# A kernel's setup joined to its main block: coefficient steps, row sums and g moved among other work

## Chip, cores and metric

One Trainium2 chip, one core of it. The metric is the device time of one execution in microseconds. Five engines with their own instruction queues work side by side: PE (matrix products), ACT, DVE and POOL (elementwise work), SP (issues the DMAs). Each queue runs strictly in order; they meet by semaphores.

## What is computed

Two graph layers with a layer norm before each, in float32, for 16 batches of 512 nodes by 128 features:

```python
h = maximum(layernorm(x), 0);  x = x + gnn0(h, adj)
h = maximum(layernorm(x), 0);  x = x + gnn1(h, W, adj)
# gnn0: eight Euler steps of an ODE
h = x0 @ fc_in_w.T + fc_in_b
f = sigmoid(alpha) * 0.5 * (adj @ h - h) + h @ (w * clip(d, 0, 1) @ w.T) - h + x0
h = h + f / 8
# gnn1: attention with 4 heads of 32, scores masked where adj == 0
```

The eight Euler steps are linear in x0. The kernel writes one step as h <- P h + h Q + x0/8, where P holds the adjacency scaled by rows and a diagonal, and Q the w part. Then h after eight steps is a sum over powers of P of terms with 128x128 coefficient matrices R_k (made by eight steps of a recurrence with Q), and a part g that comes from the bias fcb and the row sums of P's powers. The coefficients are taken three at a time, which needs P to the powers one and two as matrices and the cube P^3 for the outer steps.

## The kernel before

Every float32 matrix that enters a large product is kept as a high part (pH, u0_h, rH, wH: a copy on ACT to a shorter format) and a low part (pL, u0_l, rL, wL: a subtraction on DVE or POOL), and a product is three products: high by high, low by high, high by low. So a bank of PSUM that PE has filled is drained twice, by ACT (high) and then by DVE (low, which reads the high part).

The program has two blocks. In the first (`setup_block`, L215 to L502) each engine gets one function; the block ends when all five have ended. In the second, `ode_stage` and `attention_stage` follow each other in each engine's function. PSUM banks and SBUF of the setup are given back behind its block and used again by the ODE: ps_p0 to ps_p3 become ps_u and ps_v, ps_c and ps_w become ps_z and ps_k.

The setup, in order on PE. *Head*: transposes to keep warm (L88); the turn of w (L434); for each of four row blocks of the adjacency, which DVE scales (L367) and gives its diagonal (L369), four transposes (L439) into ps_p; then Q (L444). ACT makes the high part of P itself (p_h, L314), POOL the low part (p_l, L297). *Powers*: eight groups, n = 0 to 7, `power(1, 0..3)` and `power(2, 0..3)`. A group is twelve products (L459, L462, L465) into ps_p[m], drained by ACT (L323) and DVE (`low`, L390). Ahead of group n stands coefficient step n: n + 1 coefficients against Q, three to a product (L473) into ps_c, which DVE adds to the coefficients of the step before (`step`, L398 and L402). Among these stand the first layer norm's parts for the ODE's first four batches: on DVE the statistics (L116, L126; parts 0 and 1, in even n) and reciprocal and scaling (L138, L146; parts 2 and 3, in odd n), on ACT the root (L133, even n) and the relu with the high part of u (L200, L203, odd n), on POOL its low part (L211). DVE's order in a group is step, norm, low, and for part 3 behind low. *End*: the row sums of the powers (sixteen products with three columns, L482) in ps_w, the turns of the bias column into c_rows (L491, to ps_p[3]) and of the nine coefficient matrices (L496, to ps_p), copies s_rows (DVE), c_rows and rH (ACT) and rL (DVE), and g, the product of s_rows and c_rows (L501), which ACT copies (L342).

The ODE stage runs over groups of four batches; group 0 is written out ahead of a loop. For each batch PE makes `u_step` (four transposes of u0, L1140, then twice twelve products with the powers, L95 to L97) into three banks, which ACT and DVE drain; and one batch behind, `v_step`: products with rH and rL, to which DVE adds g (L1083). Products with the cube follow (`z_step`, `y_step`), and work for the next stage stands among them. Attention follows batch by batch.

Of the kernel before, what the change touches and what calls it, by code (L numbers as in the profile page):

```python
# [214 lines left out]
def setup_block(nc, ctx, x, adj, alpha, w, d, fcw, fcb, wqkv, keep, ln):  # L215
# [3 lines left out]

    def sem(name):  # L220
        return ctx.enter_context(nc.semaphore(name))
# [29 lines left out]
    p_done, ph_done, pl_done = (sem(n) for n in ("p_done", "ph_done", "pl_done"))  # L251
    pow_mm, pow_h, pow_l = (sem(n) for n in ("pow_mm", "pow_h", "pow_l"))
    w_mm, w_done, table_in = sem("w_mm"), sem("w_done"), sem("table_in")
    coef_mm, coef_done, coef_ready = sem("coef_mm"), sem("coef_done"), sem("coef_ready")
    r_mm, r_h, r_l = sem("r_mm"), sem("r_h"), sem("r_l")
    row_mm, row_done, g_mm, g_done = (sem(n) for n in ("row_mm", "row_done", "g_mm", "g_done"))
# [3 lines left out]

    def bank_g(t):

        return ps_c[:, t, 0:3 * D] if t < 3 else ps_p[3][:, 0:3 * D]

    block = ctx.enter_context(nc.Block())

    @block.sync
    def _(sp):
# [11 lines left out]
    @block.gpsimd  # L280
    def _(pool):
# [19 lines left out]
    @block.scalar  # L301
    def _(act):
# [5 lines left out]
        act.dma_start(d_sb[:, :], d.rearrange("(p o) -> p o", o=1)).then_inc(w_in, 16)  # L308
# [24 lines left out]
        act.wait_ge(row_mm, 2)  # L333
        act.activation(c_rows[:, :], ps_p[3][0:3, 0:3 * D], ACT.Copy).then_inc(row_done, 1)

        for j in range(3):
            act.wait_ge(r_mm, j + 1)
            act.activation(keep["rH"][:, j, :], ps_p[j][:, 0:3 * D], ACT.Copy).then_inc(r_h, 1)

# [4 lines left out]
    @block.vector  # L344
    def _(dve):
# [9 lines left out]

        dve.wait_ge(exp_done, 1)
# [5 lines left out]
        dve.wait_ge(ident_done, 2)  # L362
        for t in range(T):
# [8 lines left out]
        dve.wait_ge(w_in, 32)  # L372
# [3 lines left out]
        dve.tensor_copy(w_t[:, :], ps_w[:, 0:D])  # L376
        dve.tensor_scalar(w_td[:, :], ps_w[:, 0:D], d_dt[:, 0:1], None, ALU.mult).then_inc(w_done, 1)
        dve.wait_ge(w_mm, 2)
        dve.tensor_copy(q_sb[:, :], ps_w[:, 0:D]).then_inc(w_done, 1)

        dve.wait_ge(coef_zero, 2)
        for c in coef:
            dve.tensor_scalar(c[:, 0, 0:D], ident[:, :], DT, None, ALU.mult).then_inc(coef_ready, 1)
# [22 lines left out]

        for m in range(T):
            low(0, m)
        for n in range(STEPS):
            step(n)  # L410

            for part in (0, 1) if n % 2 == 0 else (2,):
                first_norm_dve(dve, ln, 0, n // 2, part)
            low(1 + n // T, n % T)
            if n % 2:
                first_norm_dve(dve, ln, 0, n // 2, 3)

        dve.wait_ge(qw_h, 1)
        dve.tensor_tensor(keep["wL"][:, :], w_qkv[:, :], keep["wH"][:, :].bitcast(F32),
                          ALU.subtract).then_inc(qw_l, 1)  # L420

        dve.wait_ge(row_mm, 1)
        dve.tensor_scalar(s_rows[:, :], ps_w[0:3, :], ident[0:3, 0:1], None, ALU.add).then_inc(row_done, 1)
        for j in range(3):
            dve.wait_ge(r_h, j + 1)
            dve.tensor_tensor(keep["rL"][:, j, :], ps_p[j][:, 0:3 * D], keep["rH"][:, j, :].bitcast(F32),
                              ALU.subtract).then_inc(r_l, 1)

    @block.tensor
    def _(pe):  # L430
        pe.wait_ge(ident_done, 2)
        keep_warm(pe, ps_p[0], ident, WARM_START)
        pe.wait_ge(w_in, 32)
        pe.transpose(ps_w[:, 0:D], w_sb[:, :], ident[:, :]).then_inc(w_mm, 1)  # L434

        for t in range(T):
# [5 lines left out]

        pe.wait_ge(w_done, 1)
        pe.matmul(ps_w[:, 0:D], w_td[:, :], w_t[:, :], start=True, stop=True).then_inc(w_mm, 1)  # L444
        pe.wait_ge(w_done, 2)
        pe.wait_ge(f_in, 32)
        pe.wait_ge(coef_zero, 2)
        pe.wait_ge(coef_ready, 2)

# [18 lines left out]
        for n in range(STEPS):  # L468
            if n:
                pe.wait_ge(coef_done, n)  # L470
            for s in range(1, n + 2, 3):
                k = min(3, n + 2 - s)
                mm = pe.matmul(ps_c[:, (s - 1) // 3, 0:k * CW], q_sb[:, :],  # L473
                               coef[n % 2][:, s:s + k, :].rearrange("p k c -> p (k c)"), start=True, stop=True)
            mm.then_inc(coef_mm, 1)
            power(1 + n // T, n % T)

        pe.wait_ge(pick_done, 3)
        for j in range(2):
            for m in range(T):  # L480
                for part in ("pH", "pL"):
                    mm = pe.matmul(ps_w[0:3, :], pick[:, j, :], keep[part][j][:, m, :],  # L482
                                   start=(j == 0 and m == 0 and part == "pH"),
                                   stop=(j == 1 and m == T - 1 and part == "pL"))
        mm.then_inc(row_mm, 1)

        fin = coef[STEPS % 2]
        pe.wait_ge(coef_done, STEPS)
        pe.wait_ge(pow_l, 3 * T)
        for i in range(3):  # L490
            tr = pe.transpose(ps_p[3][0:3, i * D:(i + 1) * D], fin[:, 1 + 3 * i:4 + 3 * i, D], ident[:, :])  # L491
        tr.then_inc(row_mm, 1)

        for j in range(3):
            for i in range(3):
                tr = pe.transpose(ps_p[j][:, i * D:(i + 1) * D], fin[:, 1 + 3 * i + j, 0:D], ident[:, :])  # L496
            tr.then_inc(r_mm, 1)

        pe.wait_ge(row_done, 2)
        for t in range(T):  # L500
            pe.matmul(bank_g(t), s_rows[:, t * 128:(t + 1) * 128], c_rows[:, :],  # L501
                      start=True, stop=True).then_inc(g_mm, 1)  # L502


def ode_stage(nc, ctx, sem, x, adj, x1_dram, qk_dram, v_dram, keep, ln):
# [213 lines left out]
    def sync(sp):  # L719
# [4 lines left out]
        def v_step(g, b, following):  # L724
# [3 lines left out]
            wait(sp, xv_done, GB * g + b)  # L728
            sp.dma_start(x_res[:, :, :], batch_of(x, GB * g + b).rearrange("o (p t) d -> p (o t) d", t=T)).then_inc(xr_in, 16)
# [118 lines left out]
    def scalar(act):  # L848
        def u_step(g, b, prev):
            for k in range(3):  # L850
# [148 lines left out]
    def vector(dve):  # L999
# [74 lines left out]
        def v_step(g, b, following):  # L1074
            for t in range(T):
                n = T * (GB * g + b) + t
                wait(dve, v_mm, n + 1)
                if t == 0:
# [46 lines left out]
    def tensor(pe):  # L1125
        def u_step(g, b, prev):

            nb = GB * g + b
            for k in range(3):
                n = 3 * nb + k  # L1130
                ps = u_bank(b, k)

# [15 lines left out]
        def v_step(g, b, following):  # L1148

            nb = GB * g + b  # L1150
            wait(pe, ul_done, 3 * nb + 3)
            for t in range(T):
# [413 lines left out]
def graph_block(nc, x, adj, alpha, w, d, fcw, fcb, wqkv, out):  # L1566
# [4 lines left out]
    with ExitStack() as outer:  # L1571
# [13 lines left out]
        with ExitStack() as kept:  # L1585
# [6 lines left out]
            with ExitStack() as ctx:  # L1592
                setup_block(nc, ctx, x, adj, alpha, w, d, fcw, fcb, wqkv, keep, ln)
            ode_ctx = kept.enter_context(ExitStack())
            ode = ode_stage(nc, ode_ctx, sem, x, adj, x1_dram, qk_dram, v_dram, keep, ln)
        with ExitStack() as ctx:
# [4 lines left out]
            def _(sp):  # L1601
                ode.sync(sp)
# [3 lines left out]
            def _(pool):  # L1606
                ode.gpsimd(pool)
# [3 lines left out]
            def _(act):  # L1611
                ode.scalar(act)
# [3 lines left out]
            def _(dve):  # L1616
                ode.vector(dve)
# [3 lines left out]
            def _(pe):  # L1621
                ode.tensor(pe)
# [21 lines left out]
```

## Time and profile before

| | us |
|---|---|
| median of 3 runs | 688.59 (686.69 to 688.61) |
| profiled execution | 685.76, span 684.0 |
| first block, to the first transposes of the ODE | 0 to 55.2 |
| its matrix powers on PE | 14.3 to 46.4 |
| attention | from about 390 |

The profile's times count from the first instruction of the profiled execution. In a row of the timeline, a name such as "[0.83 <-PEq L1592]" is the time that the engine sat idle ahead of the instruction and what ended it. PE's products overlap, so their durations sum to more than the time from one start to the next; starts are the better measure. The granted clock is 1.00 at 2.4 GHz and 0.50 at 1.2 GHz.

### The profile page before, as it was taken

What the parts mean: (1) busy time and instruction counts of PE and PEld (TensorE: products, weight loads), DVE (VectorE), ACT (ScalarE), POOL (GpSimd) and SP (SyncE); (2) the same over time, 40 slices, a digit from 0 to 9 for tenths busy, and PEclk for the clock granted to TensorE, in tenths of its full rate; (3) what the DMA queues carried; (4) which work ended last, traced back from release to release, by engine and by line L of the source; (5) the groups of instructions that cost most, each with busy time, mean ns of one, the idle gap of its engine ahead of it and who ended that gap; (6) DMA issues with size and microseconds to landing.
All of it is one profiled execution on the core that took longest, in us unless ns stands there. A gap on an engine that the chain in (4) does not pass through costs nothing.

```text
span 684.0 us, 13068 instructions
## 1 busy us (share of the span) xinstructions
PE 646.0 (94%) x3737; PEld 501.9 (73%) x3737; DVE 481.2 (70%) x1331; ACT 398.9 (58%) x923; POOL 130.6 (19%) x112
## 2 busy tenths in 40 slices
PE   6999999999899998999999778999999999999996
PEld 4767997789778897788987656666666666666663
DVE  6662563377833777336653569999999999999993
ACT  3433232124541345412232559999999999999994
POOL 5110235012330133301133910000000000000001
PEclk8999999999999999999999999999999999999999
DMA  3101110211235111350037896677777777777710
GB/s 111 32 0 47 32 31 16 72 40 60 75 150 170 42 58 74 147 173 13 25 109 218 181 409 191 149 180 172 175 173 177 174 176 171 177 176 177 183 58 32
DMA packets 48656, 82.53 MB, mean 121 GB/s; under 512 B 5104, under 2 KB 13680, under 8 KB 48496
## 3 DMA queue, kind: packets, MB, share of 16 engines
q1 hardware_dynamic: 48192, 82.07, 44.8%
q8 instruction: 16, 0.26, 0.2%
q14 instruction: 16, 0.13, 0.1%
q10 hardware_dynamic: 432, 0.07, 0.1%
HBM read 52.76 MB, written 29.36 MB: 120 GB/s over the span
## 4 chain that ended last, share of the span: by engine, by line
PE 30%; issue 20%; ACT 4%; POOL 4%; DVE 2%; POOLq 0%; DVEq 0%; ACTq 0%
PE ps_t L1517 13%; PE ps_o L1548 7%; PE ps_s L1532 7%; ACT v L1467 1%; ACT p_t L1458 1%; POOL z_l L831 1%; POOL h L715 1%; PE ps_o L1555 1%; POOL v L824 1%; DVE v L1489 1%; ACT ut L896 0%; DVE low L1489 0%; DVE p_t L1483 0%; PE ps_u L95 0%; PE ps_u L97 0%
## 5 line engine op out<-in xcount | busy, mean ns | idle before, releaser
L1467 ACT ACTIVATE v<-v,low 128x512 f32<-128x512 f32 x256 | 182.4, 716 | 7.0 <-DVE low L1489 6.7
L1489 DVE CUSTOM_DVE_ANT_0 v<-ps_s,pL 128x512 f32<-128x512 f32 x256 | 165.6, 685 | 11.8 <-PE ps_s L1532 11.1
L1517 PE MATMUL ps_t<-ident,v 128*128 128x128 f32 x1024 | 155.0, 274 | 4.8 <-ACT p_t L1458 4.2
L1517 PEld LDWEIGHTS ps_t<-ident,v 128*128 128x128 f32 x1024 | 123.2, 140 | 33.1 <-DVE p_t L1483 8.8
L1532 PE MATMUL ps_s<-pL,pH 128*128 128x512 f32 x256 | 122.8, 481 | 2.3 <-DVE low L1489 2.0
L1483 DVE COPY p_t<-ps_t 128x512 f32<-128x512 f32 x128 | 85.0, 685 | 0.9 <-PE ps_t L1517 0.9
L1458 ACT ACTIVATE p_t<-ps_t 128x512 f32<-128x512 f32 x128 | 74.4, 583 | 0.3 <-PE ps_t L1517 0.3
L1445 POOL TENSOR_TENSOR o_n<-o_n,x 128x512 f32<-128x512 f32 x16 | 20.6, 1286 | 265.6 <-DVE o_n L1499 265.6
L1532 PEld LDWEIGHTS ps_s<-pL,pH 128*128 128x128 f32 x256 | 48.3, 189 | 30.4 <-DVE low L1489 17.4
L95 PE MATMUL ps_v<-rH,ut 128*128 128x384 f32 x192 | 65.1, 339 | 4.6 <-DVE v L1083 4.6
L1548 PE MATMUL ps_o<-p_t,v_sb 128*32 128x512 f32 x512 | 61.4, 597 | 4.6 <-issue 3.6
L97 PE MATMUL ps_v<-rH,ut 128*128 128x384 f32 x192 | 64.6, 336 | 0.0
L96 PE MATMUL ps_v<-rL,ut 128*128 128x384 f32 x192 | 64.5, 336 | 0.0
L855 ACT ACTIVATE ut<-ps_u 128x512 fp32r<-128x512 f32 x44 | 26.1, 594 | 65.1 <-PE ps_u L97 43.6
L1008 DVE TENSOR_TENSOR ut<-ps_u,ut 128x512 fp32r<-128x512 f32 x44 | 30.3, 688 | 36.2 <-ACT ut L855 36.1
L819 POOL TENSOR_TENSOR v_l<-v,v_h 128x512 fp32r<-128x512 f32 x16 | 21.0, 1312 | 176.9 <-ACT v_h L961 176.9
L1083 DVE TENSOR_TENSOR v<-ps_v,g 128x384 f32<-128x384 f32 x64 | 35.5, 556 | 26.7 <-PE ps_v L97 25.7
L1467 ACT ACTIVATION_READ_ACCUMULATOR v<-v,low 128x1 f32 x256 | 49.2, 192 | 0.0
L95 PE MATMUL ps_u<-pH,u_h 128*128 128x512 f32 x112 | 46.0, 410 | 0.0
L97 PE MATMUL ps_u<-pH,u_l 128*128 128x512 f32 x112 | 44.3, 395 | 0.0
L96 PE MATMUL ps_u<-pL,u_h 128*128 128x512 f32 x112 | 44.2, 394 | 0.0
L961 ACT ACTIVATE v_h<-v 128x512 fp32r<-128x512 f32 x16 | 10.1, 633 | 52.8 <-DVE v L1083 52.8
(208 smaller groups left out, 1102.0 us busy)
## 6 DMA issues: line engine op xcount, KB each, us to landing
pH<-qk_dram SPq DMA_DIRECT2D x64, 256.0 KB, 6.8
pL<-qk_dram SPq DMA_DIRECT2D x64, 256.0 KB, 7.6
qk_dram<-qk SPq DMA_DIRECT2D x12, 512.0 KB, 3.3
x_ln<-in_x SPq DMA_DIRECT2D x16, 256.0 KB, 3.1
x_res<-in_x SPq DMA_DIRECT2D x16, 256.0 KB, 2.6
x_dram<-v SPq DMA_DIRECT2D x16, 256.0 KB, 3.1
v_sb<-v_dram SPq DMA_DIRECT2D x16, 256.0 KB, 9.3
x<-x_dram SPq DMA_DIRECT2D x16, 256.0 KB, 9.4
```

Of the source, the lines that this page charges most:

```text
L95: eng.matmul(psum, lh, rh, start=(first and n == 0), stop=False)
L96: eng.matmul(psum, lh, rl, start=False, stop=False)
L97: mm = eng.matmul(psum, ll, rh, start=False, stop=(last and n == len(pairs) - 1))
L1008: dve.tensor_tensor(ut_l[b % 2][:, k, :], u_bank(b, k)[:, :], ut_h[b % 2][:, k, :].bitcast(F32), ALU.subtract).then_inc(ul_done, 1)
L1083: dve.tensor_tensor(v[:, :, t, b, :], ps_v[t % 2][:, 0:3 * D].rearrange("p (j d) -> p j d", j=3), keep["g"][:, t, :].rearrange("p (j d) -> ...
L1458: act.activation(dst, src, ACT.Copy).then_inc(t_act, 1)
L1467: act.activation(s_ring[:, n % RING, :], s_ring[:, n % RING, :], ACT.Exp, bias=low[:, n:n + 1], scale=-1.0, accum_out=lsum[par][:, n:n + 1 ...
L1483: dve.tensor_copy(dst, src).then_inc(t_dve, 1)
L1489: dve.tensor_tensor_reduce(s_ring[:, n % RING, :], ps_s[S_BANK[n]][:, :], mask[:, n // HEADS, :], -SCALE, 3.0e38, ALU.add, ALU.min, low[:, ...
L1517: mm = pe.transpose(ps_t[n % T_BANKS][:, j * 128:(j + 1) * 128], s_ring[:, n % RING, j * 128:(j + 1) * 128], ident[:, :])
L1532: pe.matmul(ps_s[S_BANK[n]][:, :], q_st[par][:, h, it * 128:(it + 1) * 128], k_st[par][:, h, :], start=True, stop=True).then_inc(s_mm, 1)
L1548: mm = pe.matmul(ps_o[cols, :], v_sb[cp][:, j, cols], p_t[cp][:, hh, j, :], start=(j == 0), stop=(j == T - 1), tile_position=(0, HD * hh))
```

## The change

Setup's five programs are put ahead of the ODE's in the one block; so no engine waits for all others between them, and where memory is used twice, waits on the last user are added. On PE: w's turn waits for w alone; Q is made between row blocks two and three; coefficient steps 0 and 1 stand ahead of the powers, and step n + 2 behind group n; the row sums stand behind group 4; the turns stand behind group 6, those of the coefficients first and in ps_c, and the last group waits until ACT has copied c_rows from ps_p[3]; g is made at the head of `u_step` of the second batch. On DVE: the identity's scalings go ahead of all, the w work goes between row blocks two and three, `step(0)` stands ahead of the first low parts, and in a group the order is low, step, norm. POOL waits for all four row blocks before its first subtraction. ACT copies rH and c_rows behind the high part and root of group 6. SP's loads of the bias weights wait for one zeroed buffer only.

```diff
-        sp.wait_ge(coef_zero, 2)
+        sp.wait_ge(coef_zero, 1)
...
+        pool.wait_ge(p_done, T)
         for t in range(T):
             pool.wait_ge(ph_done, t + 1)
...
+                if (k, m) == GROUPS[COEF_AT]:
+                    for j in range(3):
+                        act.wait_ge(r_mm, j + 1)
+                        act.activation(keep["rH"][:, j, :], ps_c[:, j, 0:3 * D], ACT.Copy).then_inc(r_h, 1)
+                    act.wait_ge(row_mm, 2)
+                    act.activation(c_rows[:, :], ps_p[3][0:3, 0:3 * D], ACT.Copy).then_inc(row_done[1], 1)
...
+        rows(0)
+        rows(1)
+        dve.wait_ge(d_in, 16)
         col(dve.tensor_scalar(d_dt[:, :], d_sb[:, :], 0.0, 1.0, ALU.max, ALU.min))
...
+        rows(2)
+        rows(3)
...
+        step(0)
         for m in range(T):
             low(0, m)
-        for n in range(STEPS):
-            step(n)
-
-            for part in (0, 1) if n % 2 == 0 else (2,):
+        step(1)
+        for n, (k, m) in enumerate(GROUPS):
+            low(k, m)
+            if n + EARLY < STEPS:
+                step(n + EARLY)
+
+            for part in (0, 1) if n % 2 == 0 else (2, 3):
                 first_norm_dve(dve, ln, 0, n // 2, part)
...
+        for n, (k, m) in enumerate(GROUPS):
+            if n == len(GROUPS) - 1:
+                pe.wait_ge(row_done[1], 1)
+            power(k, m)
+            if n + EARLY < STEPS:
+                coef_step(n + EARLY)
+            if n == ROWS_AT:
+                row_sums()
+            if n == COEF_AT:
+                coef_turns()
...
+            if isinstance(g, int) and (g, b) == (0, 1):
+                keep["tensor_g"](pe)
...
+                if isinstance(g, int) and (g, b) == (0, 0):
+                    wait(pe, keep["powers"], 2 * T + k + 1)
...
             def _(pe):
+                setup.tensor(pe)
                 ode.tensor(pe)
                 attention.tensor(pe)
```

Here EARLY is 2, ROWS_AT 4 and COEF_AT 6; row_sums, coef_turns and coef_step hold the products of L482, L491 with L496, and L473.

## Rows read from the trace of the kernel before

**Rows 1.** Page, part 1: engine, busy us (share of span), instructions.

```profile
PE 646.0 (94%) x3737; PEld 501.9 (73%) x3737; DVE 481.2 (70%) x1331; ACT 398.9 (58%) x923; POOL 130.6 (19%) x112
```

**Rows 2.** Windows, ODE stage: stretch, length, busy us (instructions) by engine, granted clock, DMA.

```profile
120.00:140.00 20.00, 20.00 (x91) 16.09 (x92) 7.98 (x22) 3.19 (x7) 1.17 (x1) 1.00 0.30 93
```

**Rows 3.** Timeline, head, DVE: start, us, engine, line, operation, out<-in, shape.

```profile
6.62 0.70 DVE L367 TENSOR_SCALAR p_nat<-a_nat,s_col 128x512 f32<-128x512 f32 x1
...
7.63 1.69 DVE L367 TENSOR_SCALAR p_nat<-a_nat,s_col 128x512 f32<-128x512 f32 x1
9.35 1.24 DVE L369 SCALAR_TENSOR_TENSOR p_nat<-ident,c_col,p_nat 128x128 f32<-128x128 f32 x1
...
11.24 0.35 DVE L369 SCALAR_TENSOR_TENSOR p_nat<-ident,c_col,p_nat 128x128 f32<-128x128 f32 x1
...
12.09 0.34 DVE L377 TENSOR_SCALAR w_td<-ps_w,d_dt 128x128 f32<-128x128 f32 x1
```

**Rows 4.** One line, POOL's subtractions: ns min/median/max, first and last start.

```profile
L297 POOL TENSOR_TENSOR p_l<-p_nat,p_h x4: 1253/1386/1645, 7.5 to 12.7; 128x512 fp32r<-128x512 f32 x4
```

**Rows 5.** Timeline, the powers, all engines.

```profile
19.20 0.59 PE L473 MATMUL ps_c<-coef,q_sb 128*128 128x258 f32 x2
...
20.01 1.28 ACT L133 ACT_TABLE_LOAD   x1
...
38.97 0.59 DVE L146 TENSOR_SCALAR u<-x_ln,ln_mv,ln_std 128x128 f32<-128x128 f32 x2
...
40.26 0.63 ACT L203 ACTIVATE u_h<-u 128x512 fp32r<-128x512 f32 x1
...
40.75 0.86 DVE L116 BATCH_NORM_STATS2 ln_stat<-x_ln 128x6 f32<-128x128 f32 x4
...
41.76 0.38 DVE L126 BATCH_NORM_AGGREGATE ln_mv<-ln_stat 128x2 f32<-128x6 f32 x4
41.86 1.90 PE L473 MATMUL ps_c<-coef,q_sb 128*128 128x387 f32 x6
42.06 0.60 ACT L323 ACTIVATE pH<-ps_p 128x512 fp32r<-128x512 f32 x1 [1.16 <-PE ps_p L465]
42.55 0.29 ACT L133 ACTIVATE ln_std<-ln_mv,eps 128x4 f32<-128x4 f32 x1
42.69 0.69 DVE L390 TENSOR_TENSOR pL<-ps_p,pH 128x512 fp32r<-128x512 f32 x1 [0.55 <-ACT pH L323]
...
43.80 1.36 DVE L402 TENSOR_TENSOR coef<-ps_c,coef 128x387 f32<-128x387 f32 x3 [0.28 <-PE ps_c L473]
```

**Rows 6.** Timeline, end of the block and first ODE batch.

```profile
46.40 0.40 PE L482 MATMUL ps_w<-pH,pick 128*3 128x512 f32 x1
...
50.13 0.49 PE L491 MATMUL ps_p<-ident,coef 128*3 128x128 f32 x3
...
50.66 0.48 ACT L334 ACTIVATE c_rows<-ps_p 3x384 f32<-3x384 f32 x1 [0.90 <-PE ps_p L491]
51.05 1.20 ACT L338 ACTIVATE rH<-ps_p 128x384 fp32r<-128x384 f32 x3
...
51.53 2.20 PE L501 MATMUL ps_c<-c_rows,s_rows 3*128 3x384 f32 x6
...
55.21 0.83 PE L1140 MATMUL ps_u<-ident,u 128*128 128x128 f32 x4 [0.83 <-PEq L1592]
...
62.74 0.60 PE L1140 MATMUL ps_u<-ident,u 128*128 128x128 f32 x4
```

**Rows 7.** Windows of 1 us; the last figures are granted clock, DMA share, GB/s.

```profile
55.00:56.00 1.00, 0.79 (x5) 0.82 (x6) 0.00 (x0) 0.00 (x0) 0.00 (x0) 0.74 0.00 0
56.00:57.00 1.00, 1.00 (x4) 0.80 (x3) 0.29 (x1) 0.60 (x1) 0.00 (x0) 0.50 0.50 113
57.00:58.00 1.00, 1.00 (x4) 0.71 (x4) 0.40 (x1) 0.00 (x0) 0.00 (x0) 0.50 0.87 313
58.00:59.00 1.00, 1.00 (x4) 0.81 (x3) 0.00 (x0) 0.00 (x0) 0.00 (x0) 0.55 0.59 184
```

More of the change, by code:

```diff
@@ L212, in first_norm_pool, with setup_stage @@
                        ALU.subtract).then_inc(ln.u0l_done, 1)
-def setup_block(nc, ctx, x, adj, alpha, w, d, fcw, fcb, wqkv, keep, ln):
+def setup_stage(nc, ctx, sem, x, adj, alpha, w, d, fcw, fcb, wqkv, keep, ln):
     def sb(name, shape, dt=F32):
         return ctx.enter_context(nc.sbuf_tensor(name, shape, dt))
-    def sem(name):
-        return ctx.enter_context(nc.semaphore(name))
     a_nat = sb("a_nat", [128, T, N])
@@ L278, in _, with gpsimd @@
                 sp.dma_start(w_qkv[:, :], wqkv).then_inc(q_in, 16)
-    @block.gpsimd
-    def _(pool):
+    def gpsimd(pool):
         pool.memset(ln.norm.eps[:, :], EPS).then_inc(ln.eps_done, 1)
@@ L299, in _, with scalar @@
             first_norm_pool(pool, ln, 0, b)
-    @block.scalar
-    def _(act):
+    def scalar(act):
         act.dma_start(alpha_sb[:, :], alpha.rearrange("(p t) -> p t", t=T)).then_inc(alpha_in, 16)
@@ L307, in _ @@
         act.dma_start(w_sb[:, :], w).then_inc(w_in, 16)
-        act.dma_start(d_sb[:, :], d.rearrange("(p o) -> p o", o=1)).then_inc(w_in, 16)
+        act.dma_start(d_sb[:, :], d.rearrange("(p o) -> p o", o=1)).then_inc(d_in, 16)
         act.wait_ge(alpha_in, 16)
@@ L331, in _, with scalar_g @@
                     first_norm_act(act, ln, 0, n // 2)
[L333 to L338, printed above, removed]
+                if (k, m) == GROUPS[COEF_AT]:
[4 more added lines that the diff above has]
+                    act.activation(c_rows[:, :], ps_p[3][0:3, 0:3 * D], ACT.Copy).then_inc(row_done[1], 1)
+    def scalar_g(act):
         for t in range(T):
@@ L342, in _, with vector @@
             act.activation(keep["g"][:, t, :], bank_g(t), ACT.Copy).then_inc(g_done, 1)
-    @block.vector
-    def _(dve):
+    def vector(dve):
         n_col = 0
@@ L353, in col @@
             dve.wait_ge(col_done, n_col)
+        dve.wait_ge(ident_done, 2)
+        dve.wait_ge(coef_zero, 2)
+        for c in coef:
+            dve.tensor_scalar(c[:, 0, 0:D], ident[:, :], DT, None, ALU.mult).then_inc(coef_ready, 1)
         dve.wait_ge(exp_done, 1)
@@ L360, in _, with rows @@
         col(dve.tensor_scalar(c_col[:, :], s_col[:, :], -1.0, 1.0 - DT, ALU.mult, ALU.add))
-        dve.wait_ge(ident_done, 2)
-        for t in range(T):
+        def rows(t):
             dve.wait_ge(adj_in[t], 16)
@@ L405, in step, with tensor, rows @@
             last.then_inc(coef_done, 1)
+        step(0)
         for m in range(T):
             low(0, m)
-        for n in range(STEPS):
-            step(n)
-            for part in (0, 1) if n % 2 == 0 else (2,):
-                first_norm_dve(dve, ln, 0, n // 2, part)
[L414 to L430, printed above, removed]
+        step(1)
[4 more added lines that the diff above has]
+            for part in (0, 1) if n % 2 == 0 else (2, 3):
+                first_norm_dve(dve, ln, 0, n // 2, part)
+            if n == ROWS_AT:
+                dve.wait_ge(row_mm, 1)
+                dve.tensor_scalar(s_rows[:, :], ps_w[0:3, :], ident[0:3, 0:1], None, ALU.add).then_inc(row_done[0], 1)
+                dve.wait_ge(qw_h, 1)
+                dve.tensor_tensor(keep["wL"][:, :], w_qkv[:, :], keep["wH"][:, :].bitcast(F32),
+                                  ALU.subtract).then_inc(qw_l, 1)
+            if n == COEF_AT:
+                for j in range(3):
+                    dve.wait_ge(r_h, j + 1)
+                    dve.tensor_tensor(keep["rL"][:, j, :], ps_c[:, j, 0:3 * D], keep["rH"][:, j, :].bitcast(F32),
+                                      ALU.subtract).then_inc(r_l, 1)
+    def tensor(pe):
         pe.wait_ge(ident_done, 2)
         keep_warm(pe, ps_p[0], ident, WARM_START)
-        pe.wait_ge(w_in, 32)
+        pe.wait_ge(w_in, 16)
         pe.transpose(ps_w[:, 0:D], w_sb[:, :], ident[:, :]).then_inc(w_mm, 1)
-        for t in range(T):
+        def rows(t):
             pe.wait_ge(p_done, t + 1)
@@ L441, in _, with coef_step @@
                     tr.then_inc(pow_mm, 1)
+        def coef_step(n):
+            if n:
+                pe.wait_ge(coef_done, n)
+            for s in range(1, n + 2, 3):
+                k = min(3, n + 2 - s)
+                mm = pe.matmul(ps_c[:, (s - 1) // 3, 0:k * CW], q_sb[:, :],
+                               coef[n % 2][:, s:s + k, :].rearrange("p k c -> p (k c)"), start=True, stop=True)
+            mm.then_inc(coef_mm, 1)
+        rows(0)
+        rows(1)
         pe.wait_ge(w_done, 1)
         pe.matmul(ps_w[:, 0:D], w_td[:, :], w_t[:, :], start=True, stop=True).then_inc(w_mm, 1)
+        rows(2)
+        rows(3)
         pe.wait_ge(w_done, 2)
@@ L448, in _ @@
         pe.wait_ge(coef_ready, 2)
+        coef_step(0)
+        coef_step(1)
         def power(k, m):
@@ L466, in power @@
             mm.then_inc(pow_mm, 1)
[L468 to L491, printed above, removed]
@@ L492, in _, with row_sums @@
-        tr.then_inc(row_mm, 1)
-        for j in range(3):
-            for i in range(3):
-                tr = pe.transpose(ps_p[j][:, i * D:(i + 1) * D], fin[:, 1 + 3 * i + j, 0:D], ident[:, :])
-            tr.then_inc(r_mm, 1)
-        pe.wait_ge(row_done, 2)
+        def row_sums():
+            pe.wait_ge(pick_done, 3)
+            pe.wait_ge(pow_l, 2 * T)
+            for j in range(2):
+                for m in range(T):
+                    for part in ("pH", "pL"):
+                        mm = pe.matmul(ps_w[0:3, :], pick[:, j, :], keep[part][j][:, m, :],
+                                       start=(j == 0 and m == 0 and part == "pH"),
+                                       stop=(j == 1 and m == T - 1 and part == "pL"))
+            mm.then_inc(row_mm, 1)
@@ new lines, in coef_turns @@
+        def coef_turns():
+            fin = coef[STEPS % 2]
+            pe.wait_ge(coef_done, STEPS)
+            for j in range(3):
+                for i in range(3):
+                    tr = pe.transpose(ps_c[:, j, i * D:(i + 1) * D], fin[:, 1 + 3 * i + j, 0:D], ident[:, :])
+                tr.then_inc(r_mm, 1)
+            pe.wait_ge(pow_l, 2 * T)
+            for i in range(3):
+                tr = pe.transpose(ps_p[3][0:3, i * D:(i + 1) * D], fin[:, 1 + 3 * i:4 + 3 * i, D], ident[:, :])
+            tr.then_inc(row_mm, 1)
@@ L500, in _, with tensor_g @@
+        for n, (k, m) in enumerate(GROUPS):
[4 more added lines that the diff above has]
+                coef_step(n + EARLY)
+            if n == ROWS_AT:
+                row_sums()
+            if n == COEF_AT:
+                coef_turns()
+    def tensor_g(pe):
+        for s in row_done:
+            pe.wait_ge(s, 1)
         for t in range(T):
+            if t < 3:
+                pe.wait_ge(r_l, t + 1)
@@ L501, in _ @@
             pe.matmul(bank_g(t), s_rows[:, t * 128:(t + 1) * 128], c_rows[:, :],
                       start=True, stop=True).then_inc(g_mm, 1)
+    keep["scalar_g"], keep["tensor_g"], keep["g_done"] = scalar_g, tensor_g, g_done
+    keep["powers"], keep["weights"] = pow_l, [(r_l, 3), (qw_l, 1)]
+    keep["adj_read"] = (p_done, T)
+    return Programs(sync, gpsimd, scalar, vector, tensor)
 def ode_stage(nc, ctx, sem, x, adj, x1_dram, qk_dram, v_dram, keep, ln):
@@ L728, in v_step @@
             wait(sp, xv_done, GB * g + b)
+            if isinstance(g, int) and (g, b) == (0, 0):
+                wait(sp, *keep["adj_read"])
             sp.dma_start(x_res[:, :, :], batch_of(x, GB * g + b).rearrange("o (p t) d -> p (o t) d", t=T)).then_inc(xr_in, 16)
@@ L849, in u_step @@
         def u_step(g, b, prev):
+            if isinstance(g, int) and (g, b) == (0, 1):
+                keep["scalar_g"](act)
             for k in range(3):
@@ L1077, in v_step @@
                 wait(dve, v_mm, n + 1)
+                if t == 0 and isinstance(g, int) and (g, b) == (0, 0):
+                    wait(dve, keep["g_done"], T)
                 if t == 0:
@@ L1128, in u_step @@
             nb = GB * g + b
+            if isinstance(g, int) and (g, b) == (0, 1):
+                keep["tensor_g"](pe)
             for k in range(3):
@@ L1131, in u_step @@
                 ps = u_bank(b, k)
+                if isinstance(g, int) and (g, b) == (0, 0):
+                    wait(pe, keep["powers"], 2 * T + k + 1)
                 if (b, k) == (0, 2):
@@ L1151, in v_step @@
             wait(pe, ul_done, 3 * nb + 3)
+            if isinstance(g, int) and (g, b) == (0, 0):
+                wait(pe, keep["powers"], 3 * T)
+                for s, value in keep["weights"]:
+                    wait(pe, s, value)
             for t in range(T):
@@ L1592, in graph_block @@
             with ExitStack() as ctx:
-                setup_block(nc, ctx, x, adj, alpha, w, d, fcw, fcb, wqkv, keep, ln)
+                setup = setup_stage(nc, ctx, sem, x, adj, alpha, w, d, fcw, fcb, wqkv, keep, ln)
             ode_ctx = kept.enter_context(ExitStack())
@@ L1601, in _ @@
             def _(sp):
+                setup.sync(sp)
                 ode.sync(sp)
@@ L1606, in _ @@
             def _(pool):
+                setup.gpsimd(pool)
                 ode.gpsimd(pool)
@@ L1611, in _ @@
             def _(act):
+                setup.scalar(act)
                 ode.scalar(act)
@@ L1616, in _ @@
             def _(dve):
+                setup.vector(dve)
                 ode.vector(dve)
```

24 lines of the change are left out of this document (12 added, 12 removed).

## The prediction

> **What bounds the kernel now.** I read the busy shares first. TensorE (PE) is busy 94% of the span [rows 1], and a stretch of the ODE stage shows it full while DVE, ACT and POOL are not [rows 2]. So up to the attention stage PE's order sets the time, and what PE loses or wins in the setup is carried to the end one for one, as far as I can read. The change touches only the first 63 us, so I read the timeline there, engine by engine. The reader is to see three things in it. In the head, DVE scales the rows of the adjacency, and the third and fourth row block take 1.69 and 1.24 us for what takes 0.70 and 0.35 elsewhere, while POOL is in its four subtractions [rows 3, 4]. In the matrix powers PE has no gap: 27.20 us pass from 19.20 to 46.40 [rows 5, 6]. At the end come PE's row sums, turns and g, then 0.83 us of idle PE at the end of the block [rows 6], and then the granted clock is 0.74, 0.50, 0.50 and 0.55 in the microseconds from 55 to 59, that is, at the 1.2 GHz level from 55.5 to 58.9 [rows 7].
>
> Two marks carry the comparison: PE is free behind the first group of powers at 19.20 (call this zero), and the second batch of the ODE begins at 62.74 [rows 5, 6]. Between them lie 43.54 us of PE. From 41.86 to 46.40 stand eight coefficients and a group, from 19.20 to 46.40 thirty-five and seven groups; that gives 0.215 us for a coefficient and 2.8 for a group. So the 43.54 are: coefficients 7.5, seven groups 19.6, row sums 3.73 (46.40 to 50.13), turns 1.40 (50.13 to 51.53), g 2.85, idle 0.83, and 7.53 for the first batch's products, of which 3.4 us at half clock lost 1.7.
>
> **Head: gain 1.8.** POOL now waits for all four row blocks, so DVE's two slow steps lose 0.99 + 0.89 = 1.88 us. Four small operations on d and w (0.92 us: from 11.51, by the view 0.27 behind the start of the last diagonal step, to 12.43) come in between. The fourth row block, at 11.59 before, is done at 11.59 - 1.88 + 0.92, about 10.6 [rows 3]. POOL then does its four subtractions in a row, at 1.25 us or a little more each (the shortest of [rows 4]); with one DVE step between, they end at about 15.9. The group's first products can begin at about 13.3, behind the first coefficient step and the first low part, but its eighth needs the last subtraction. Five products follow from 15.9, at 0.23 us (2.8 / 12) at full clock or nearly twice that at half, so PE is free at 17.1 to 18.0. Upper bound: at half clock throughout, 13.35 + 12 x 0.43 = 18.5. I take 17.4, a gain of 1.8 (0.7 to 2.1). The two scalings of the identity go ahead of DVE's first wait and cost nothing there; the earlier loads on SP's queue are awaited later than they land.
>
> A page that bears here is the Trainium skill's SBUF — State Buffer, section "Who interferes with whom": a DVE operation that uses the pair of ports shared with GpSimd locks it for a whole instruction, and the loser waits it out. The slow steps above agree. By that rule the copy at the head of the first coefficient step would wait out a subtraction too and take a turn of 0.2 us between two; without it the gain of the head would be about 2.0.
>
> **The powers: cost 1.1, less 0.4.** One coefficient step is now ahead of zero, so 0.43 us go (2 x 0.215). Otherwise PE has the same products in another order. What is new is the order on DVE and ACT: the norm's parts stand behind the low part and the coefficient step of the same group, not ahead of the low part. From zero, with durations of rows 5: high part 0.2 to 0.8; low 1.44; step 2.04; statistics and aggregate 1.39, to 3.43. ACT now waits for that before its root. Its function table load (1.28) stands directly ahead of the root, behind the wait in program order; no row shows a load against an unmet wait, so its price is between 0 and 1.28, and I take all of it. Root done at 5.05; the second high part at 5.0, though PE had finished at 3.44. Then low and step 7.0, reciprocal and four scalings 8.3, relu and high part of u (0.67 + 0.63) 9.65. Third group: PE done at 7.1, its high part at 9.65, step done at 11.9. PE's next coefficient step, due at 11.0, waits for that: 0.9 lost. The fourth high part is done at 14.05, just late for the fifth group: 0.15. Behind that the row sums give DVE and ACT 3.73 us to catch up. Bounds 0 to 1.5; I take 1.1 for the three together with 0.03 of waiting before.
>
> **The seventh group: cost 4.6 and 1.5.** Here the moved work makes a new wait. The last group may not start until ACT has copied c_rows out of its bank, and PE makes c_rows' turns only behind the seventh group (index 6). ACT is late: the relu and high part for the third batch keep it until 1.34 behind the end of that group (28.7). From 30.06: high part 0.60, low part 0.61 to its successor, statistics and aggregate of the fourth batch 1.39, root 0.3, the three rH copies (1.17 to the next), c_rows 0.48, with handovers 4.6, to 34.66 [rows 5, 6]. PE has its twelve turns (1.33) in that time and is done at 30.04. It waits 4.62 us. Behind ACT's wait for the root stand rH and c_rows; behind rH stands DVE's rL; PE has nothing else in its queue. The order alone sets a floor: were ACT free at once, 3.4 would be left; doubling of the lateness gives 6.
>
> The clock fell after 0.83 us of idle PE in the trace [rows 6, 7], and stayed up in the gapless powers. Behind 4.6 idle us I take it down again, for a time like the one read, with 1.5 lost in the last group (0 to 3.4, that is none or twice the 1.7 read). TensorE: Matmul & The Clock Gate, section "HAM oscillation — how this bites in real kernels", of the Trainium skill says that a wait between bursts of matmuls throttles the next burst. The trace agrees (0.83 us idle, then half clock); without that rule and row the 1.5 would be 0.
>
> **End of the block and ODE: gain 2.8.** The idle 0.83 goes. The first batch's products follow the last group at once, at full clock or nearly: 5.83 in place of 7.53. g (2.6 for 2.85) comes behind them. ACT reaches the first batch's copies only behind the fourth batch's relu, about 4.2 us behind the last group, but PE needs a drained bank only for the second batch, 8.4 behind it; so 2 us of cover are left, and if g were faster or ACT later, the difference would be paid. g's copies on ACT (four of about 0.5) are needed by the first addition on DVE, two batches of products later. The x loads of SP go out earlier and are needed later.
>
> **Sum.** 7.1 + 19.6 + 1.1 + 3.73 + 1.33 + 4.62 + 1.5 + 5.83 + 2.6 = 47.4 in place of 43.5: 3.9 more, 1.8 less at the head: 2.1 us longer. The profiled execution took 685.76 (span 684.0 and 1.8 around it), so 687.9 by that basis; it was faster than all runs shown (median 688.59). I add the difference to the median: 690.7.
>
> **Rivals.** First, not slower: DVE and ACT keep up. Place: the table load and ACT's relu of the third batch; price 1.1 (the stalls in the powers) and 1.2 (the lateness at the seventh group). It decides if ACT has finished that relu before group seven ends. For it: DVE and ACT are idle much of the powers in the present order. Against: the chain of low, step, statistics and root is serial. It gives 2.1 - 2.3, so 688.4; with the clock staying up too, 686.9. Second, worse: g's three-row products, now amid the ODE, bring the clock down once more. For it: the fall at 55.5 came behind them, with only 0.83 idle. Against: full products now stand right behind them. It costs 1.7: 692.4; with the row sums doing the same in the powers, 694.1. Third, the join is worth more than its visible idle, because the block's end also holds back engines that the PE view does not show; ODE then would run 2 to 3 us ahead of my sum and the kernel would be faster, 685.9 at best. I see no row that says so. Last, the join hides nothing, because ACT's lateness reaches the second batch: 2 us of cover would have to go; 692 or so.
>
> **Chances.** My forecast (689 to 692) 0.45; the first rival 0.27; the second and the last together 0.18; the third 0.10. This kernel's measurements tell about 0.3% (2.06 us) from no change. My forecast lies on that edge, so it goes half to slower, half to same. Faster 0.13 (the third and a little of the first), same 0.46, slower 0.41. Range: 685.8 (the first rival with the clock up, and most of the third) to 695.0 (the second with both falls, and the upper bound of the head); the forecast's own 689 to 692.
>
> **What would show it.** In the trace of the changed kernel: DVE's four row scalings at 0.70, POOL's first subtraction behind the fourth; PE free behind the first group near 17.4; an idle PE of 4 to 5 us between the turns and the last group's products, released by ACT's c_rows; half clock right behind it; no gap between last group and first ODE transposes. The second batch's transposes at 64.8 confirm the sum. I am wrong if that idle is under 3 us, if c_rows comes ahead of the fourth batch's root, or if stretches behind 65 us change in length.

## The result and the profile after

The changed kernel took 691.39 us (median of 4, 690.31 to 692.07) against 688.43 for the kernel before: ratio 1.0047, 95% interval 1.0025 to 1.007. It is 3.0 us (0.5%) slower. The profiled execution took 690.31 (span 688.5) against 685.76 (684.0), so 4.5 us longer; both lie below their medians, the one of before by more.

The page's first part answers to [rows 1]: the same instructions, hardly other busy times.

```profile
PE 648.7 (94%) x3737; PEld 503.1 (73%) x3737; DVE 481.3 (70%) x1331; ACT 398.2 (58%) x923; POOL 130.0 (19%) x112
```

The head, in DVE's timeline rows and POOL's and PE's, answers to [rows 3, 4]:

```profile
8.27 0.67 DVE L372 TENSOR_SCALAR p_nat<-a_nat,s_col 128x512 f32<-128x512 f32 x1
...
8.97 0.35 DVE L374 SCALAR_TENSOR_TENSOR p_nat<-ident,c_col,p_nat 128x128 f32<-128x128 f32 x1
...
10.40 4.98 POOL L298 TENSOR_TENSOR p_l<-p_nat,p_h 128x512 fp32r<-128x512 f32 x4 [6.45 <-DVE p_nat L374]
10.44 1.32 DVE L403 COPY coef<-coef 128x129 f32<-128x129 f32 x1
...
12.61 2.26 PE L481 MATMUL ps_p<-pH,p_h 128*128 128x512 f32 x4
...
16.94 0.81 PE L455 MATMUL ps_c<-coef,q_sb 128*128 128x387 f32 x2
```

The row blocks are back at 0.67 and 0.35, and PE is free behind the first group at 16.94 instead of 19.20. The group began at 12.61; in the kernel before it began at 14.95:

```profile
14.95 2.07 PE L459 MATMUL ps_p<-pH,p_h 128*128 128x512 f32 x4
...
16.00:17.00 1.00, 1.00 (x4) 0.81 (x3) 1.00 (x5) 0.00 (x0) 0.00 (x0) 0.50 0.00 0
```

It took about as long in both, 4.33 and 4.25 us, and in both the granted clock (the third figure from the end of a row of windows) was 0.50 for most of it: from 11.1 to 17.9 before, from 12.1 to 15.5 in the changed kernel:

```profile
14.00:15.00 1.00, 1.00 (x4) 0.81 (x3) 1.00 (x2) 0.00 (x0) 1.00 (x2) 0.50 0.00 0
```

In the powers (the view of [rows 5]) the reader is to see the table load, which begins only when DVE's aggregate ends ACT's wait, and two of the waits of PE that follow from ACT being late:

```profile
20.45 1.28 ACT L133 ACT_TABLE_LOAD   x1 [2.72 <-DVE ln_mv L126]
...
28.94 1.57 PE L455 MATMUL ps_c<-coef,q_sb 128*128 128x387 f32 x4 [0.67 <-DVE coef L407]
...
31.05 0.19 PEld L481 LDWEIGHTS ps_p<-pH,p_h 128*128 128x128 f32 x1 [0.28 <-ACT pH L323]
```

At the seventh group (the views of [rows 5, 6]) ACT's and DVE's queues are one serial chain, and PE stands at its end:

```profile
46.56 0.63 ACT L203 ACTIVATE u_h<-u 128x512 fp32r<-128x512 f32 x1
46.84 0.49 PE L512 MATMUL ps_p<-ident,coef 128*3 128x128 f32 x3
47.09 0.58 ACT L323 ACTIVATE pH<-ps_p 128x512 fp32r<-128x512 f32 x1
47.70 0.69 DVE L395 TENSOR_TENSOR pL<-ps_p,pH 128x512 fp32r<-128x512 f32 x1 [1.84 <-ACT pH L323]
48.31 0.86 DVE L116 BATCH_NORM_STATS2 ln_stat<-x_ln 128x6 f32<-128x128 f32 x4
49.32 0.38 DVE L126 BATCH_NORM_AGGREGATE ln_mv<-ln_stat 128x2 f32<-128x6 f32 x4
49.73 0.30 ACT L133 ACTIVATE ln_std<-ln_mv,eps 128x4 f32<-128x4 f32 x1 [2.06 <-DVE ln_mv L126]
49.94 1.23 ACT L336 ACTIVATE rH<-ps_c 128x384 fp32r<-128x384 f32 x3
51.05 0.46 ACT L338 ACTIVATE c_rows<-ps_p 3x384 f32<-3x384 f32 x1
51.56 2.07 PE L481 MATMUL ps_p<-pH,p_h 128*128 128x512 f32 x4 [4.23 <-ACT c_rows L338]
...
56.70 0.60 PE L1186 MATMUL ps_u<-ident,u 128*128 128x128 f32 x4
...
62.70 2.20 PE L532 MATMUL ps_c<-c_rows,s_rows 3*128 3x384 f32 x6
...
65.47 0.66 PE L1186 MATMUL ps_u<-ident,u 128*128 128x128 f32 x4
...
73.07 0.34 PE L95 MATMUL ps_v<-rH,ut 128*128 128x384 f32 x1
```

The first product of v, at 73.07, stood at 68.67 before: 4.4 of the 4.5 us between the spans are lost by then. The granted clock ([rows 7] before) falls twice more, in the wait and behind g:

```profile
49.00:50.00 1.00, 0.00 (x0) 0.00 (x0) 0.56 (x5) 0.27 (x2) 0.00 (x0) 0.83 0.00 0
...
56.00:57.00 1.00, 1.00 (x6) 0.81 (x5) 0.00 (x0) 0.10 (x1) 0.00 (x0) 0.75 0.00 0
...
66.00:67.00 1.00, 1.00 (x6) 0.80 (x5) 0.20 (x1) 0.67 (x2) 0.00 (x0) 0.87 0.00 0
67.00:68.00 1.00, 1.00 (x4) 0.79 (x3) 0.49 (x1) 0.00 (x0) 0.00 (x0) 0.50 0.00 0
...
70.00:71.00 1.00, 1.00 (x5) 0.82 (x4) 0.00 (x0) 0.49 (x1) 0.00 (x0) 0.93 0.00 0
```

### The profile page after: what moved, and what is told of

Its sections match the earlier page's. It is cut to its first block, busy times and chain, and to the rows that moved or that the text cites. A ratio compares the mean times of both kernels' runs of the same rounds, so it can differ in the third digit from the quotient of the medians.

```text
span 688.5 us, 13067 instructions
## 1 busy us (share of the span) xinstructions
PE 648.7 (94%) x3737; PEld 503.1 (73%) x3737; DVE 481.3 (70%) x1331; ACT 398.2 (58%) x923; POOL 130.0 (19%) x112
## 4 chain that ended last, share of the span: by engine, by line
PE 31%; issue 20%; ACT 4%; POOL 4%; DVE 2%; POOLq 0%; DVEq 0%; ACTq 0%
PE ps_t L1567 13%; PE ps_o L1598 7%; PE ps_s L1582 7%; ACT p_t L1508 1%; POOL z_l L869 1%; ACT v L1517 1%; POOL h L751 1%; PE ps_o L1605 1%; POOL v L862 1%; DVE v L1539 1%; ACT ut L936 0%; DVE low L1539 0%; DVE p_t L1533 0%; PE ps_u L95 0%; PE ps_u L97 0%
## 5 line engine op out<-in xcount | busy, mean ns | idle before, releaser
L1582 PEld LDWEIGHTS ps_s<-pL,pH 128*128 128x128 f32 x256 | 48.4, 189 | 30.4 <-DVE low L1539 17.4
```

The source lines that it names most:

```text
L1582: pe.matmul(ps_s[S_BANK[n]][:, :], q_st[par][:, h, it * 128:(it + 1) * 128], k_st[par][:, h, :], start=True, stop=True).then_inc(s_mm, 1)
```

## The experiments

All start from the changed kernel. "Mark" is the start of the first product of v in the profiled execution (68.67 before, 73.07 changed). Medians from different batches of runs are compared through their ratio to the kernel before (688.2, 688.3 and 687.7 in the three batches).

**1. c_rows in another bank.**

```diff
-                    act.activation(c_rows[:, :], ps_p[3][0:3, 0:3 * D], ACT.Copy).then_inc(row_done[1], 1)
+                    act.activation(c_rows[:, :], ps_w[0:3, 0:3 * D], ACT.Copy).then_inc(row_done[1], 1)
...
-            pe.wait_ge(pow_l, 2 * T)
+            pe.wait_ge(row_done[0], 1)
...
-                tr = pe.transpose(ps_p[3][0:3, i * D:(i + 1) * D], ...)
+                tr = pe.transpose(ps_w[0:3, i * D:(i + 1) * D], ...)
...
-            if n == len(GROUPS) - 1:
-                pe.wait_ge(row_done[1], 1)
             power(k, m)
```

> c_rows is turned into the bank of the row sums (free once s_rows is copied), so the last group of powers waits for no copy. My account (the changed kernel loses its time in front of the last group): the 4.2 us of idle PE ahead of that group go, and with them the half clock that follows (2.3 us of 5.1 for the group); the first product of v, at 73.07 in the changed kernel, comes at about 66.5, and the median falls by some 6.5 us to about 685. ACT is still late, but PE needs a drained bank only two batches' products later. Rival A (joining the blocks costs something else, such as slower work side by side): the median falls by under 2 us. Rival B (ACT's lateness only moves on to the next bank that it must drain): an idle PE of 2 to 4 us shows up in the first ODE batch and the median stays above 688.

Median 684.99, ratio 0.9967 (0.9949 to 0.9985). PE goes from the turns to the last group without a gap, and that group takes 2.88 us (46.74 to 49.62) at full clock:

```profile
46.50 0.49 PE L512 MATMUL ps_w<-ident,coef 128*3 128x128 f32 x3
46.74 1.18 PE L481 MATMUL ps_p<-pH,p_h 128*128 128x512 f32 x4
...
49.62 0.60 PE L1184 MATMUL ps_u<-ident,u 128*128 128x128 f32 x4
```

The mark is at 65.97, 7.1 earlier (0.3 of it already at zero). ACT still copies c_rows at 50.70, but nothing waits for it. So the loss stood in front of the last group and in that group's slower clock; the fall behind g is still there (58.4 to 61.8). Rivals A and B are out.

**2. Warm products in the wait.**

```diff
                 coef_turns()
+                pe.wait_ge(row_done[0], 1)
+                keep_warm(pe, ps_w, ident, 34)
```

> 34 transposes of the identity (about 0.11 us each, 3.7 us) stand in PE's wait ahead of the last group; nothing waits for them and the wait itself stays. It separates the clock from the wait. If the half clock in the last group comes from PE's idleness, that group takes 2.8 us in place of 5.1, its first product is still at about 51.6, and the median falls by about 2.3 us to 689. If the fall of the clock has another cause, the group still takes 5.1 us and the median stays at 691.

Median 689.15, ratio 1.0012 (0.9997 to 1.0028). The wait's end, counted from zero (16.58 here), is where it was, 34.6 us behind it, and the last group takes 2.9 us in place of 5.1:

```profile
46.77 3.88 PE L88 MATMUL ps_w<-ident 128*128 128x128 f32 x34
51.16 1.20 PE L481 MATMUL ps_p<-pH,p_h 128*128 128x512 f32 x4 [0.52 <-ACT c_rows L338]
...
54.06 0.60 PE L1188 MATMUL ps_u<-ident,u 128*128 128x128 f32 x4
...
62.00:70.00 8.00, 8.00 (x38) 6.38 (x37) 1.74 (x3) 2.92 (x6) 0.00 (x0) 1.00 0.00 0
```

The half clock in that group came from PE's idleness and cost 2.2 us in this pair of executions. Here the clock did not fall behind g either (the last row), and the mark is at 68.81.

**3. The norm ahead of the low part.**

```diff
+            for part in (0, 1) if n % 2 == 0 else (2, 3):
+                first_norm_dve(dve, ln, 0, n // 2, part)
             low(k, m)
             if n + EARLY < STEPS:
                 step(n + EARLY)
-
-            for part in (0, 1) if n % 2 == 0 else (2, 3):
-                first_norm_dve(dve, ln, 0, n // 2, part)
```

> In each group DVE does the norm's parts ahead of the low part and the coefficient step, as the kernel before did; all else as in the changed kernel. My account (ACT waits for its root because the norm stands behind the low part, and everything behind the root in ACT's queue is late): the stalls of PE in the powers (0.3, 0.7 and 0.3 us) go, the wait ahead of the last group falls from 4.2 to about 1.4 us (high part, root, three rH copies and c_rows less the twelve turns), and the clock may then stay up (2.3). The median falls by 4 to 6.5 us, to 685 to 687. Rival (the norm ahead delays the low parts and so PE): PE stalls in the powers for the low parts, and the median falls by under 2 us.

Median 684.49, ratio 0.9946 (0.9929 to 0.9963), 6.9 below the changed kernel and a little past my range. PE has no wait left in the powers, and the one ahead of the last group is 1.04:

```profile
45.05 0.29 ACT L133 ACTIVATE ln_std<-ln_mv,eps 128x4 f32<-128x4 f32 x1
45.24 1.24 ACT L336 ACTIVATE rH<-ps_c 128x384 fp32r<-128x384 f32 x3
46.35 0.46 ACT L338 ACTIVATE c_rows<-ps_p 3x384 f32<-3x384 f32 x1
```
```profile
46.87 1.20 PE L480 MATMUL ps_p<-pH,p_h 128*128 128x512 f32 x4 [1.04 <-ACT c_rows L338]
```

The root follows the high part at once; nothing in it waits for DVE now. The rival is out: the low parts were not missed.

**4. The table early.**

```diff
                 act.activation(keep["wH"][:, :], w_qkv[:, :], ACT.Copy).then_inc(qw_h, 1)
+                act.activation(table2[:, :], ln.norm.eps[:, :], ACT.Sqrt).then_inc(table_in, 1)
```

> One small square root on ACT ahead of the powers brings the function table in while ACT is idle; nothing else changes. My account: in the changed kernel the load stands behind the wait for the first aggregate and makes ACT 1.3 us late for three groups; with it gone PE's three stalls in the powers (1.3 us together) go and the seventh group ends 1.3 earlier, while the wait ahead of the last group stays at 4.2, because the row sums had let ACT catch up by then. Median 690, first product of v 71.8. Rival: PE's stalls in the powers come from the order on DVE alone; then they stay above 0.8 us.

Median 688.29, ratio 1.0008 (0.9995 to 1.0021), 1.7 below what I expected. In the trace the load runs at 13.25, in a stretch in which ACT has nothing else to do; the waits in the powers are gone, and the twelve turns begin 1.8 earlier (44.07 for 45.86), of which 0.3 stood at zero already. The wait ahead of the last group stays (the second row):

```profile
13.25 1.28 ACT L322 ACT_TABLE_LOAD   x1
...
49.80 2.07 PE L483 MATMUL ps_p<-pH,p_h 128*128 128x512 f32 x4 [4.26 <-ACT c_rows L340]
```

The clock came back earlier in that group here (it took 4.2 us), and the mark is at 70.38. So the waits in the powers came from the load and DVE's order together, not from that order alone; each of the two edits, this and the one before, removes them.

**5. g spread.** The products of g, one ahead of each of the second batch's three products of u and one at the head of v:

```diff
-            if isinstance(g, int) and (g, b) == (0, 1):
-                keep["tensor_g"](pe)
             for k in range(3):
+                if isinstance(g, int) and (g, b) == (0, 1):
+                    keep["tensor_g"](pe, k)
```

> The changed kernel with g's four products no longer in one piece: one ahead of each of the second batch's three products of u, the last at the head of the first batch's v; ACT's copies follow them. The wait ahead of the last group stays. If the three-row products standing in one piece bring the clock down behind them (66.7 to 70.1 in the changed kernel), the second batch runs at full clock and the first product of v comes 1.6 us earlier, at about 71.5; median 689.8. If the fall is a late effect of something else, it stays, and so does the median, 691.4.

Median 692.39, ratio 1.0052 (1.0033 to 1.0071): no gain. The clock stayed up behind g, as my account had it, but it also did so in experiments 2 and 6 with g in one piece, so this execution alone does not decide. The mark is at 72.85, only 0.2 earlier. The expectation missed a price: a piece by itself takes more than its share of the 2.77 us that the four take in a row (the rows of experiment 7 show it), 1.1 us in all. And the half clock behind the wait lasted into the first batch here, which took 6.46 us in place of 6.00.

**6. POOL does not wait.**

```diff
-        pool.wait_ge(p_done, T)
```

> The changed kernel without POOL's wait for all four row blocks: POOL's subtractions start behind the first row block again, as in the kernel before. My account of the head: DVE's third and fourth row block take 1.9 us longer again, POOL's last subtraction ends earlier, and the first group is now held by the low parts and not by POOL; PE is free behind it 1 to 2 us later (16.7 in the changed kernel, 18 to 18.7 here); median 692.5 to 693. Rival: the wait was worth nothing, since what it gives DVE it takes from POOL's last subtraction; then PE is free at 16.7 again or earlier, and the median stays at 691.4 or below.

Median 691.68, ratio 1.0068 (1.0041 to 1.0096). The diagonal step is slow again, the scaling hardly:

```profile
8.22 0.86 DVE L371 TENSOR_SCALAR p_nat<-a_nat,s_col 128x512 f32<-128x512 f32 x1
9.11 1.24 DVE L373 SCALAR_TENSOR_TENSOR p_nat<-ident,c_col,p_nat 128x128 f32<-128x128 f32 x1
```

PE is free behind the first group at 17.42, 0.5 later than with the wait (16.94), in two executions whose clock was down over the same stretch of the head (12.1 to 15.5). The 16.6 of the five variants above is no measure for it, since the clock was up in their heads. Both accounts missed: I had 18 to 18.7, the rival 16.7. The w work between the row blocks hides most of one subtraction (the third block's scaling starts at 8.22 and takes 0.86, where it started at 7.63 and took 1.69 before). The medians don't settle half a microsecond.

**7 to 9. All four edits, and g in one, two or four pieces.**

> The changed kernel with c_rows in the other bank, the norm ahead of the low part, the early table and g spread. If the terms found so far add up (wait 4.2, half clock behind it 2.3, stalls in the powers 1.3, half clock behind g 1.6), the first product of v comes at 73.1 - 9.4, about 63.7, and the median is 682, 6 below the kernel before. Rival: the terms cover each other, because PE meets the next wait (ACT's drains in the first two batches); then the first product of v is at 65 or later and the median no better than the 684.5 of the norm's move alone.

> As the kernel with all four edits, but g in one piece as in the changed kernel. If g in one piece brings the clock down, the first product of v is 1.6 us later than with g spread (about 65.3) and the granted clock shows 0.50 for some 3 us behind g; median 683.6. If it does not, both agree within 0.3 us.

> As the kernel with all four edits, but g in two pieces of two products: one ahead of the second batch, one at the head of the first batch's v. From the first batch's transposes to the first product of v the kernels took 14.75 us with g in one piece and the clock up, 16.35 or 17.92 with one piece and the clock down behind it, and 15.83 with g in four pieces (each piece costs about 0.25 more, and the clock stayed up). If the pieces cost by their number and two products are too short to bring the clock down, this one takes about 15.3 and the median is 682. If two products still bring it down, it takes 16.5 or more and the median is 683 or above.

| g | median | ratio to before (95%) | first batch to mark | mark |
|---|---|---|---|---|
| four pieces (7) | 682.46 | 0.9922 (0.9905 to 0.994) | 15.83 | 64.79 |
| one piece (8) | 682.77 | 0.9914 (0.9894 to 0.9934) | 17.92 | 67.05 |
| two pieces (9) | 682.62 | 0.9925 (0.9899 to 0.995) | 15.04 | 63.16 |

The last column holds 0.8 to 1.0 us more in the first two, whose heads ran at half clock for longer (PE free at 17.5 and 17.6; 16.6 in the third). All three beat the kernel before by 5 to 6 us and the changed kernel by nearly 9. So the terms do not cover each other: with all four edits 8.3 us of the 9.4 expected came at the mark, although 0.5 was lost at the head and 1.1 in the pieces of g. The clock was up behind g with four pieces and two; with one it fell, while g was still running (57.3 to 64.1, by the windows), and that cost 3.2 us against the 14.75 of the two one-piece executions in which it stayed up (experiments 2 and 6). Experiment 8's clock at both ends of the fall:

```profile
57.00:58.00 1.00, 1.00 (x4) 0.22 (x2) 0.00 (x0) 0.70 (x2) 0.00 (x0) 0.66 0.00 0
...
64.00:65.00 1.00, 1.00 (x5) 0.81 (x4) 0.00 (x0) 0.48 (x1) 0.00 (x0) 0.93 0.00 0
```

In four pieces (experiment 7) the timeline of PE shows the price of a change between kinds of products:

```profile
54.96 0.91 PE L532 MATMUL ps_c<-c_rows,s_rows 3*128 3x384 f32 x2
55.80 0.66 PE L1188 MATMUL ps_u<-ident,u 128*128 128x128 f32 x4
...
56.39 0.91 PE L532 MATMUL ps_c<-c_rows,s_rows 3*128 3x384 f32 x2
57.22 0.50 PE L95 MATMUL ps_u<-pH,u_h 128*128 128x512 f32 x1
```

A piece takes 0.84 us to the next product, where one of four in a row takes 0.69; with what stands around it, the four cost 1.1 more in all (15.83 less 14.75). In six runs of each the three medians lie within 0.3 us, so which is best stays open.

## Why the prediction was right, point by point

**Head.** Forecast 17.4, measured 16.94, a gain of 2.3 in place of 1.8, a little past my bound. The forecast let POOL's last subtraction set this time. POOL did its part, and 0.5 earlier (done at 15.4, not 15.9; ACT's first exponential stood at 4.38 for 4.58). But in this execution PE did not wait for it: at half clock it came to its eighth product only at 15.8. With the clock up (experiments 1 to 5) PE waits 0.7 us for POOL there and is free at 16.6; in experiment 2:

```profile
15.31 0.51 PE L484 MATMUL ps_p<-pH,p_l 128*128 128x512 f32 x1 [0.73 <-POOL p_l L298]
```

So the wait that I named is real, and its place in the changed kernel's own profile was taken by the clock; that 16.94 lies so near 17.4 is in part luck. By the Trainium skill's SBUF — State Buffer, "Who interferes with whom", I had expected DVE's copy at the head of the coefficient step to wait out a subtraction of POOL. The trace agrees: the copy took 1.32 us beside the first subtraction, and 0.22 elsewhere.

**Powers.** Forecast 28.7 us from zero to the turns, measured 28.9. PE's three waits in it sum to 1.27 (0.32, 0.67, 0.28), where I had 1.1 in other shares (0.03, 0.9, 0.15). Taking the whole table load behind the wait was right; the trace shows the load released by the aggregate.

**The wait.** Forecast 4.62, measured 4.23, by the chain as written down: high part, low part, statistics, root, three copies, c_rows. Experiments 1 and 3 undo it from both ends, by its bank and by its order.

**The clock behind it.** In the profiled execution this term was mis-sized: forecast 1.5, measured 2.2 by experiment 2. PE was idle for 4.2 us and the clock stayed at 1.2 GHz nearly through the whole group (to 56.5), where the trace of before had it at half for 3.4 us. The size varies: the same wait stands in experiments 4, 5 and 6, and there the last group took 4.2, 5.3 and 4.5 us against 2.9 at full clock, so 1.3, 2.4 and 1.6 lost. TensorE: Matmul & The Clock Gate, "HAM oscillation — how this bites in real kernels" in the Trainium skill, says that such a wait throttles the products behind it. The trace agrees with the fall (0.50 from 50 us on).

**End and ODE.** First batch 6.0 (forecast 5.83), g 2.77 (2.6), mark of the second batch 65.47 (64.8). ACT's late drains were covered, as forecast: no variant shows a wait of PE for them up to the mark.

**The second rival** held beside the forecast and not in its place: the clock fell behind g and cost 1.67 in the second batch (7.60 for 5.93). I gave it the right price (1.7) and too small a chance; it fell in five of the seven executions that have g in one piece inside the ODE. The forecast had let the 1.7 us of half clock go together with the 0.83 us of idle PE at the block's end. In the kernel before that idle stood right behind g; here g has no idle beside it, and the same 1.7 came back behind g. So this part of the gain at the end was not there in the profiled execution, and one of my own signs of being wrong came true: a stretch behind 65 us changed in length.

With that, the profile's sum would have been 2.1 + 1.7 + 0.6 of smaller errors (the last group's clock the largest, the head against it), the 4.4 at the mark. The medians moved by 3.0, between that and the 2.1 of the forecast. That the median came within 0.7 us of the 690.7 is in part luck: the falls of the clock come and go from one execution to the next. The mean granted clock was 0.981 to 0.987 in the four runs of the changed kernel and 0.980 to 0.990 in those of the kernel before, and of each only one execution was profiled.

**The first rival** (DVE and ACT keep up) is out as a description, and right as a recipe: experiment 3 makes them keep up, and the change becomes a gain. The third rival, a hidden gain of the join, found no support, and the last, a lost cover, did not occur.

From the mark to the end of the span it is 615.3 us before and 615.4 in the changed kernel, so nothing there explains the loss. The variants take 615.4 to 618.6, and that goes with the number of falls of the clock behind the mark: one fall (at the start of attention; in experiment 6 in the ODE) goes with 615.3 to 616.3 us, two (experiments 2, 3 and 9) with 617.0 to 617.6, three (experiment 5) with 618.6. A mark that comes earlier is therefore not seen in full in the span of a single execution: experiment 9's stands 3.9 us ahead of experiment 8's, its span is 1.6 us shorter.

## What to carry to other kernels

When work is moved behind other work, follow each in-order queue to the copy that gives the bank back: here a 0.46 us copy of three rows stood behind a root and three copies that it does not need, and PE behind the copy. Put what waits for nothing new (the norm) ahead of what waits, choose a bank with no early next user, and let a function table load while its engine is idle. Such a wait is paid twice, by its length and by the slower clock behind it. Before two profiled executions are compared, count the falls of the clock in each: here one more or less was worth 1.3 us or more.

## What the runs showed of the hardware that was not expected

- g's four products (three rows each, eight passes on PE in a row, 2.8 us), with full products ahead and behind and no idle PE, went with a fall to half clock right behind them, or still within them, in five of seven executions, for 3.4 or 6.8 us. Cut into pieces of one or two products they did not in three executions. Three are few, and why it varies wasn't tried.
- Cutting g has a price: from the first batch to the mark it took 14.75 us in one piece with the clock up, 15.04 in two pieces, 15.83 in four.
- The same idle is not always followed by half clock. Two idle stretches of PE, 2.04 us each, one ending between 173 and 183 us and one between 260 and 270, stand in the ODE stage of all eleven profiled executions. Half clock followed within 1.5 us behind three of the 22 (experiments 5, 6 and 9).
- In the head the clock was down from 11.1 to 17.9 us in the kernel before, from 12.1 to 15.5 in the changed kernel and experiment 6, not at all in experiments 1 to 5 and 9, and from 9.5 to 16.3 in the variants with g in four pieces and in one. PE was free behind the first group at 16.94 in the changed kernel, 16.6 with the clock up, and 17.5 and 17.6 with the long half clock. PE's wait for POOL at full clock hides most of a short half clock, not of a long one.
